# Projecting the first half of the queries before the second half is normalised, with the split of the weights shared by two engines

## The reference

```
x: (8, 128, 512)                      # 8 tiles of 128 tokens, 1024 tokens in all
xn = (x - mean(x)) / sqrt(var(x) + 1e-5)
q  = xn @ Wq                          # Wq: (512, 1024), so q: 1024 tokens x 1024
kv = context @ Wkv                    # Wkv: (512, 2048)
x  = x + softmax(clip(mask(q k^T / 8))) v @ Wo + bo
```

## Time and profile before

| what | value |
|---|---|
| runs | 3358.84, 3362.94, 3366.79 us (median 3362.94) |
| profiled execution | 3363.22 us, span 3361.2 us |
| PE, DVE, ACT, POOL busy | 93%, 74%, 51%, 52% of the span |
| mean granted clock of TensorE | 0.97 of full speed |

### The profile page before, as it was taken

One profiled execution on the slowest core, in us unless ns is written; L12 is line 12 of the kernel. 1 busy time (PEld: TensorE's weight loads), 2 busy tenths in 40 slices (PEclk: granted clock), 3 DMA queues, 4 the chain that ended last, 5 costly groups with the idle time before them and its releaser, 6 DMA issues. The chain is left out here.

```text
span 3361.2 us, 50813 instructions
## 1 busy us (share of the span) xinstructions
PE 3135.3 (93%) x18068; PEld 2664.4 (79%) x18068; DVE 2480.7 (74%) x3447; ACT 1728.2 (51%) x3283; POOL 1744.6 (52%) x1122
## 2 busy tenths in 40 slices
PE   5999999999999999999999996988989877899996
PEld 4788888888888888888888885867767655678996
DVE  4699999999999999999999996685675754523213
ACT  3466666666666666666666663253453426211000
POOL 4365665566556566566555664141441436346663
PEclk9999999999999999999999997989999889899998
DMA  5544444454454445444454444100000120123220
GB/s 195 157 119 111 117 116 113 117 129 98 120 123 121 114 105 127 109 123 115 102 129 117 113 101 116 57 28 28 1 16 1 58 62 1 63 70 125 83 88 32
DMA packets 216084, 312.41 MB, mean 93 GB/s; under 512 B 28704, under 2 KB 122016, under 8 KB 207648
## 3 DMA queue, kind: packets, MB, share of 16 engines
q1 hardware_dynamic: 213024, 300.74, 34.3%
q0 software_dynamic: 2816, 8.46, 0.7%
HBM read 151.75 MB, written 23.13 MB: 52 GB/s over the span
## 5 line engine op out<-in xcount | busy, mean ns | idle before, releaser
L480 POOL TENSOR_TENSOR es<-es,e 128x512 f32<-128x512 f32 x480 | 621.7, 1295 | 741.6 <-ACT e L556 741.6
L645 DVE TENSOR_TENSOR e_hl<-e,e_hl 128x512 fp32r<-128x512 f32 x512 | 679.7, 1327 | 0.3 <-ACT e L556 0.3
L489 POOL TENSOR_TENSOR c_lo<-raw,c_hi 128x512 fp32r<-128x512 f32 x248 | 427.0, 1722 | 0.0
L636 DVE TENSOR_SCALAR sc<-ps_s,top 128x512 f32<-128x512 f32 x512 | 384.6, 751 | 55.7 <-ACT e L556 1.4
L715 PEld LDWEIGHTS ps_s<-q_hl,k_hl 128*128 128x128 f32 x2048 | 308.6, 190 | 67.7 <-issue 28.5
L632 DVE TENSOR_TENSOR ps_s<-ps_s,right 128x512 f32<-128x512 f32 x512 | 353.4, 690 | 9.1 <-ACT right L565 7.8
L715 PE MATMUL ps_s<-q_hl,k_hl 128*128 128x256 f32 x2048 | 330.9, 284 | 15.4 <-DVE sc L636 15.4
L665 PE MATMUL ps_p<-c_hi,wa 128*128 128x512 f32 x1024 | 339.1, 392 | 4.5 <-PEq L115 4.5
L665 PE MATMUL ps_p<-wa,c_hi 128*128 128x512 f32 x1024 | 337.8, 391 | 0.0
L676 PE MATMUL ps_o<-e_hl,v_hl 128*128 128x256 f32 x2048 | 331.1, 284 | 3.3 <-DVE e_hl L645 3.3
L552 ACT ACTIVATE e_hl<-sc 128x512 fp32r<-128x512 f32 x512 | 324.7, 634 | 1.4 <-PE ps_o L676 1.0
(11 more groups left out here) (395 smaller groups left out, 7371.7 us busy)
## 6 DMA issues: line engine op xcount, KB each, us to landing
k_hl<-ot SPq DMA_DIRECT2D x1024, 128.0 KB, 2.8
raw<-in_ctx_t SPq DMA_DIRECT2D x64, 1024.0 KB, 6.4
raw<-in_L_ffn_W_experts SPq DMA_DIRECT2D x64, 256.0 KB, 2.9
q_hl<-q_hi_scratch SPq DMA_DIRECT2D x32, 256.0 KB, 5.5
q_hl<-q_lo_scratch SPq DMA_DIRECT2D x32, 256.0 KB, 6.3
raw<-in_L_xattn_Wkv SPq DMA_DIRECT2D x8, 512.0 KB, 4.9
q_hi_scratch<-qa_qh SPq DMA_DIRECT2D x16, 256.0 KB, 2.5
q_lo_scratch<-qa_ql SPq DMA_DIRECT2D x16, 256.0 KB, 3.4
```

Source lines behind the costliest of these rows:

```text
L480: g.tensor_tensor(ES[:, GL], ES[:, GL], e, ALU.add).then_inc(summed, 1)
L489: g.tensor_tensor(C_lo[:, n % 2, k, :], RAW[:, n % 2, k, :], C_hi[:, n % 2, k, :].bitcast(F32), ALU.subtract).then_inc(clo_done, 1)
L636: v.tensor_scalar(SC[:, s % 2].rearrange("p (j q) -> p j q", j=GRP), halves[:, :, 0, :], top[:, i * (M // P) + kt16:i * (M // P) + kt16 + ...
L645: v.tensor_tensor(E2[:, s % 2, :, 1, :], E[:, s % 2].rearrange("p (j q) -> p j q", j=GRP), E2[:, s % 2, :, 0, :].bitcast(F32), ALU.subtrac ...
```

## The change

In `stage_queries`:
- VectorE's program becomes: first half (`norms(0)`, `turned_lo(0)`), the low part of Wq piece 1 (which was GpSimd's), `norms(1)`, low parts of query groups 0 and 1, `turned_lo(1)`, groups 2 to 15.
- TensorE transposes tiles 0 to 3, computes groups 0 and 1, transposes tiles 4 to 7, and computes groups 2 to 15. `qa_pst` and `qa_psq` have four banks each.
- ScalarE puts its copies in a matching order, and the splits of pieces 4 to 7 stand after groups 3, 5, 8 and 10 (before: after 0, 2, 4 and 6).
- On SyncE's queue the loads of pieces 4 to 7 stand after the stores of groups 0, 2, 5 and 7 (before: 4 and 5 ahead of all stores, 6 after store 1, 7 after store 3).

In `rsqrt_cols`, for all stages: one instruction more ahead of the refinements, and three instead of four in each refinement, or two where y has a single column.

```
-    for n in range(3):
-        c.link(v.tensor_tensor(tmp, y, y, ALU.mult))
-        c.link(v.tensor_tensor(tmp, tmp, x, ALU.mult))
-        c.link(v.tensor_scalar(tmp, tmp, -0.5, 1.5, ALU.mult, ALU.add))
-        c.link(v.tensor_tensor(y, y, tmp, ALU.mult))
+    c.link(v.tensor_scalar(x, x, -0.5, None, ALU.mult))
+    for n in range(3):
+        if y.shape[-1] == 1:
+            c.link(v.scalar_tensor_tensor(out=tmp, in0=y, scalar=y, in1=x, op0=ALU.mult, op1=ALU.mult))
+        else:
+            c.link(v.tensor_tensor(tmp, y, y, ALU.mult))
+            c.link(v.tensor_tensor(tmp, tmp, x, ALU.mult))
+        c.link(v.scalar_tensor_tensor(out=y, in0=tmp, scalar=1.5, in1=y, op0=ALU.add, op1=ALU.mult))
...
+        QR, QB, HB = 3, 4, B // 2
...
+        SPLIT_LOADS = {0: 4, 2: 5, 5: 6, 7: 7}
+        SPLITS = {3: 4, 5: 5, 8: 6, 10: 7}
+        TURNS_AFTER = 1
...
             def load(n):
-                if n >= 2:
-                    sp.wait_ge(lo_split, n - 1)
+                if n == 3:
+                    sp.wait_ge(wq_lo_second, 1)
+                elif n >= 2:
+                    sp.wait_ge(lo_split, max(n - 2, 1))
...
-            for n in range(2, 6):
-                load(n)
-            store(0)
-            store(1)
-            load(6)
-            store(2)
-            store(3)
-            load(7)
-            for n in range(4, NQ):
+            load(2)
+            load(3)
+            for n in range(8):
+                store(n)
+                if n in SPLIT_LOADS:
+                    load(SPLIT_LOADS[n])
+            for n in range(8, NQ):
                 store(n)
...
         def _(g):
-            for n in range(NP):
+            for n in (0, *range(2, NP)):
...
+            norms(0)
+            turned_lo(0)
+            v.wait_ge(hi_split, 2)
+            for hi, lo, src in parts_of(1):
+                v.tensor_tensor(lo, src, hi.bitcast(F32), ALU.subtract).then_inc(wq_lo_second, 1)
+            norms(1)
             for n in range(NQ):
                 v.wait_ge(hi_done, n + 1)
...
+                if n == TURNS_AFTER:
+                    turned_lo(1)
...
             split(0)
+            turned_hi(0)
+            turned_hi(1)
             split(1)
-            for b in range(B):
-                turned_hi(b)
+            turned_hi(2)
+            turned_hi(3)
             split(2)
             split(3)
...
-                if n in (0, 2, 4, 6):
-                    split(4 + n // 2)
+                if n == TURNS_AFTER:
+                    for b in range(HB, B):
+                        turned_hi(b)
+                if n in SPLITS:
+                    split(SPLITS[n])
...
+            turn(0)
+            t_.wait_ge(lo_split, 1)
+            t_.wait_ge(wq_lo_second, 1)
             for n, (c, t) in enumerate(GROUPS):
-                if n >= 2:
-                    t_.wait_ge(lo_done, n - 1)
+                t_.wait_ge(xt_lo, (t + 1) * HB)
+                if n >= QB:
+                    t_.wait_ge(lo_done, n - QB + 1)
...
+                if n == TURNS_AFTER:
+                    turn(1)
```

More of the change, by code:

```diff
@@ L129, in stage_queries @@
         QL_ = sb("ql", [P, QR, 512], F32R)
[L130 to L131 removed]
+        ps_t = ctx.enter_context(nc.psum_tensor("qa_pst", [P, HB, 512], F32))
+        ps_q = ctx.enter_context(nc.psum_tensor("qa_psq", [P, QB, 512], F32))
         ident_in, raw_in, x_in = sem("ident_in"), [sem("raw_in0"), sem("raw_in1")], [sem(f"x_in{b}") for b in range(B)]
[L134 removed]
+        hi_split, lo_split, wq_lo_second = sem("hi_split"), sem("lo_split"), sem("wq_lo_second")
         vchain, normed, turned, xt_hi, xt_lo = sem("vchain"), sem("normed"), sem("turned"), sem("xt_hi_done"), sem("xt_lo_done")
@@ L208, in _, with norms @@
             c = Chain(v, vchain, 0, 0)
-            for hb in range(2):
-                bs = range(hb * HB, (hb + 1) * HB)
+            def norms(hb):
+                bs, s_ = range(hb * HB, (hb + 1) * HB), slice(hb * HB, (hb + 1) * HB)
                 for b in bs:
@@ L218, in _, with turned_lo @@
                     v.tensor_scalar(X[:, b], X[:, b], mom[:, b, 0:1], rs[:, 1, b:b + 1], ALU.subtract, ALU.mult).then_inc(normed, 1)
-                for b in bs:
+            def turned_lo(hb):
+                for b in range(hb * HB, (hb + 1) * HB):
                     v.wait_ge(xt_hi, b + 1)
                     t_ = slice(b * P, (b + 1) * P)
-                    v.tensor_tensor(XT_lo[:, :, t_], ps_t[:, b % 2].rearrange("p (k f) -> p k f", k=KC), XT_hi[:, :, t_].bitcast(F32),
+                    v.tensor_tensor(XT_lo[:, :, t_], ps_t[:, b % HB].rearrange("p (k f) -> p k f", k=KC), XT_hi[:, :, t_].bitcast(F32),
                                     ALU.subtract).then_inc(xt_lo, 1)
+            norms(0)
[4 more added lines that the diff above has]
+            norms(1)
             for n in range(NQ):
                 v.wait_ge(hi_done, n + 1)
-                v.tensor_tensor(QL_[:, n % QR, :], ps_q[:, n % 2, :], QH[:, n % QR, :].bitcast(F32), ALU.subtract).then_inc(lo_done, 1)
+                v.tensor_tensor(QL_[:, n % QR, :], ps_q[:, n % QB, :], QH[:, n % QR, :].bitcast(F32), ALU.subtract).then_inc(lo_done, 1)
+                if n == TURNS_AFTER:
+                    turned_lo(1)
         @block.scalar
@@ L237, in turned_hi @@
                 a.wait_ge(turned, b + 1)
-                a.copy(XT_hi[:, :, b * P:(b + 1) * P], ps_t[:, b % 2].rearrange("p (k f) -> p k f", k=KC)).then_inc(xt_hi, 1)
+                a.copy(XT_hi[:, :, b * P:(b + 1) * P], ps_t[:, b % HB].rearrange("p (k f) -> p k f", k=KC)).then_inc(xt_hi, 1)
             split(0)
+            turned_hi(0)
+            turned_hi(1)
             split(1)
-            for b in range(B):
-                turned_hi(b)
+            turned_hi(2)
+            turned_hi(3)
             split(2)
@@ L248, in _ @@
                     a.wait_ge(q_out[n % QR], 32 * (n // QR))
-                a.copy(QH[:, n % QR, :], ps_q[:, n % 2, :]).then_inc(hi_done, 1)
-                if n in (0, 2, 4, 6):
-                    split(4 + n // 2)
+                a.copy(QH[:, n % QR, :], ps_q[:, n % QB, :]).then_inc(hi_done, 1)
+                if n == TURNS_AFTER:
[3 more added lines that the diff above has]
+                    split(SPLITS[n])
         @block.tensor
@@ L255, in _, with turn @@
             t_.wait_ge(ident_in, 16)
[L256 to L264, removed]
+            def turn(hb):
+                for b in range(hb * HB, (hb + 1) * HB):
+                    t_.wait_ge(normed, b + 1)
+                    if b >= HB:
+                        t_.wait_ge(xt_lo, b - HB + 1)
+                    for k in range(KC):
+                        mm = t_.transpose(ps_t[:, b % HB, k * P:(k + 1) * P], X[:, b, k * P:(k + 1) * P], I[:])
+                    mm.then_inc(turned, 1)
+            turn(0)
+            t_.wait_ge(lo_split, 1)
+            t_.wait_ge(wq_lo_second, 1)
             for n, (c, t) in enumerate(GROUPS):
-                if n >= 2:
-                    t_.wait_ge(lo_done, n - 1)
+                t_.wait_ge(xt_lo, (t + 1) * HB)
+                if n >= QB:
+                    t_.wait_ge(lo_done, n - QB + 1)
                 m = 0
@@ L270, in _ @@
                     for w, x_ in ((WQ_lo, XT_hi), (WQ_hi, XT_lo), (WQ_hi, XT_hi)):
-                        mm = t_.matmul(ps_q[:, n % 2, :], w[:, k, c * P:(c + 1) * P], x_[:, k, t * 512:(t + 1) * 512],
+                        mm = t_.matmul(ps_q[:, n % QB, :], w[:, k, c * P:(c + 1) * P], x_[:, k, t * 512:(t + 1) * 512],
                                        start=m == 0, stop=m == 3 * KC - 1)
```

3 lines of the change are left out of this document (removed).

## The result

The change took 3338.28 us (median of 4 runs, 3334.97 to 3341.87) against 3362.81 us of the kernel before (4 runs, 3358.84 to 3366.79): a ratio of 0.9928, interval 0.9914 to 0.9943, so 24.5 us (19 to 29) faster. The prediction had 3345.3 and a range of 3339 to 3354, so the measured time lies 0.7 us outside it. The profiled execution took 3334.97 us, its span is 3333.0 us, 28.2 less than before's. The next stage's first matmul stands at 83.19 instead of 98.40: 15.2 us come from the first stage, where 14.7 were forecast. The other 13.0 us lie behind it, where step 5 had 3.2.

What follows compares the result with a forecast made beforehand. TensorE, busy 93% of the span, was taken as the bound, so gains come only where it stands still. 14.7 us (first stage) plus 3.2 (rsqrt_cols elsewhere) made 17.9: 3363.2 - 17.9 = 3345.3 us, range 3339 to 3354.

Steps and rivals of the forecast that it cites:

- step 5: Shorter rsqrt_cols in later stages: ten wide calls at 0.2 us, two narrow at 0.6; 3.2 us saved, bounds 0 and 5.8.
- Step 1: First stage, first half: without GpSimd's second subtraction VectorE goes on; tile 3 normalised at about 17.1, low part ends 19.75.
- Step 2: First stage: Wq piece 1's low part on VectorE takes 2.3 us; group 0 starts at 22.1, 17.2 us earlier.
- Step 3: First stage, second half: GpSimd's subtractions lock VectorE's normalising chain, costing 6.2 us; TensorE waits from 30.2 to 35.6.
- Step 4: First stage, groups 2 to 15: four banks keep stalls to 1.0 us; body ends at 79.2, 14.7 us saved.
- The lock bit: Rival, first stage's second half: the lock bites less, 3 to 5 us more gained, 3340 to 3342; 17%.
- the later loads: Rival, groups 2 to 15: later loads or stores hold ScalarE, 4 to 9 us lost, 3349 to 3354; 19%.
- the body did not stretch: Rival, first stage: head shortened but body stretches by as much; within 6.7 us of before; 6%.
- the clock rival: First stage: clock stays at 1.2 GHz after TensorE's pause; all 14 groups cost 34 us, net slower (3379); 4%.

Runs made afterwards that it cites:

- e6: The change with the low part of Wq piece 1 back on GpSimd, order of halves, banks and queues kept; 3333.2 us (0.9915).
- e4: The change with GpSimd taking piece 2 only when all 8 tiles are normalised; 3332.3 us (0.9914).
- e5: The change with two PSUM banks instead of four for the query groups (QB = 2); 3341.6 us (0.9949).
- e7: The kernel before with the new rsqrt_cols in every stage but the first; 3351.0 us, gain 8 us (4 to 12).
- e12: The kernel before with the new rsqrt_cols in all later stages but stage_attend; 3350.4 us, gain 6 us (3 to 9).
- e2: The kernel before with the new rsqrt_cols alone, in all stages; 3352.7 us (0.9973).
- e9: e4 with GpSimd's first subtraction (Wq piece 0) also waiting, until the first half is normalised; 3325.1 us (0.9902).
- e15: e9 run again, unchanged; 3329.0 us (0.9907).

## Why the prediction was right where it was, and wrong in the size

*Step 1, first half.* Right: the normalising ended at 16.9 (forecast 17.1), the low parts at 19.4 (19.75).

*Step 2, piece 1 on VectorE.* The cost was right (2.28 us, forecast 2.3), group 0 at 21.74 (22.1). The gain came, 17.6 us for the 17.2 forecast, but not by the move: e6 starts group 0 at 21.31 without it. Step 1 wanted GpSimd's second subtraction gone so that VectorE could go on; in e6 it ran, and VectorE's low parts began at 16.81 all the same, as in the change (16.85).

*Step 3, the lock on the second half.* Right in size, partly wrong in kind. The pause was 5.93 us and ended at 36.13 (forecast 5.4 us, ending at 35.6). e4, without it, is 8.7 us faster in the stage, where the step had 5.4: there TensorE also transposes at full pace, 1.9 instead of 3.7 us, and the matmuls behind them run at full pace (0.23 us apart from the second on). Wrong was which instructions are held. The step took all four with one tensor input as free, from a row of a single column. With four columns they are not: L220 took 1.21 and L77 2.32 us beside GpSimd. The chain was held four times, not three. It cost little, since what counts is when GpSimd's last subtraction ends: 34.1 (forecast 33.6). The Trainium skill, page "SBUF — State Buffer", section "Who interferes with whom", says that tensor_scalar too can enter a mode that takes the port pair shared with GpSimd; these two rows agree with it, and the 0.15 of the single column would fit its not being entered there; no row names the mode.

*Step 4, groups 2 to 15.* Right: the last group's matmul at 78.3 (body end 78.7, forecast 79.2), no stall of TensorE where 1.0 was allowed. The reason given, the four banks, was too strong as far as e5's profile goes: ScalarE waited 2.1, 0.4 and 1.6 us for the pieces in the change, and with two banks TensorE stalled for 1.3 us.

*Step 5, `rsqrt_cols` elsewhere.* This is the step that failed: 3.2 us, where the rows give 5.6. It is a term that was mis-sized. The new form, `scalar_tensor_tensor`, was costed by a row of 0.227 us. In the change it takes 0.16 us where its scalar is a constant; only the other kind, whose scalar is a column of memory, takes 0.22:

```profile
2073.41 0.16 DVE L86 SCALAR_TENSOR_TENSOR t_col<-t_col 128x1 f32<-128x1 f32 x1
2073.61 0.22 DVE L82 SCALAR_TENSOR_TENSOR t_col<-t_col 128x1 f32<-128x1 f32 x1
```

A wide call therefore loses two instructions of 0.20 each, 0.4 us and not 0.2. A one-column refinement takes 0.45 us (two in 0.90, from 2073.16 to 2074.06) instead of 0.77 (two in 1.54): 0.8 a call with the instruction more ahead of it, and not 0.6. The wait in `stage_front` shows just that, 3.9 us for two calls and now 2.3. So 10 x 0.4 + 2 x 0.8 = 5.6 us, close to the step's upper bound of 5.8, and the measured idle time says 5.8. Choosing the row by its operation's name, when the one in the earlier trace rows has another kind of scalar, cost 2.4 us of the forecast.

That the totals agree so well is in part luck. Stage by stage, from the first matmul of one to that of the next, TensorE's idle time (mean of the four profiles without the new code there less that of the nine with it) fell by 0.8 us in `stage_dense`, as worked out (2 x 0.4), by 0.9 in `stage_front` (1.6) and 0.9 in `stage_project` (1.6), by nothing in `stage_attend` (0.4) and by 0.2 in `stage_cross` (no call), but by 3.0 in `stage_ffn_attend` (1.2). There a wait that the step did not list, for ScalarE, is shorter; before, then the change:

```profile
PE g_ps L1743 <- ACT g_s L1600: 5.9, 1, 5.9
```

```profile
PE g_ps L1769 <- ACT g_s L1626: 4.3, 1, 4.3
```

It is 5.9 or 6.0 us in all six profiles with the old code in that stage, and 4.4 or less in all eleven with the new. What shortens it by 1.6 us no run here shows.

*The sum.* The forecast is 7.0 us above the measured median: 2.4 to 2.6 from step 5, 0.5 from the first stage (15.2 for 14.7), 0.4 because the sum started from the profiled 3363.2 and not from the median, and 3.5 for which the sum has no term. Step 5 at its right size would have made it 3342.9, inside the range; the 3.5 us took it below 3339. The 21.0 us that the first stage and step 5 account for lie inside the measured interval of 19 to 29. The sum put the clock behind the first stage at nothing, and TensorE's busy time there scatters by 6 us for one kernel; the profiled pair had 5.9 us of it. Whether the change also runs a little longer at full clock is open: the means of the profiles say up to 4.8 us, most of it due to which executions were profiled, and the intervals of the parts (e7, e12) ask for none.

*The rivals.* The lock bit as forecast; the later loads held ScalarE for 4.1 us in three waits and TensorE for none, where the rival had 4 to 9 lost; the body did not stretch. After the pause of 5.93 us TensorE was at half pace for the transposes, and so were the first four matmuls behind them (0.57 to 0.42 apart); all 168 of the 14 groups took 39.2 us, 0.233 each against 0.227 at full pace, so the clock rival did not come true.

## What to carry to other kernels

When two engines lock each other out for a whole instruction, a chain of tiny dependent instructions is the worst thing to put beside long ones: each 0.16 us link can cost 2.3. Holding the long instructions back with a wait until the chain is done costs nothing if their results have slack: here two such waits gave 7 to 9 us, and moving work between the two engines gave nothing. Before crediting a moved piece of work, check that what waited for it was not waiting for something else anyway. And when a profile pair differs over a long stretch, split the stretch into TensorE's idle and busy time: in these 17 profiles the idle time went with the code, and the busy time of the same matmuls with the clock, which scatters.

## What the runs showed of the hardware beyond that

- A one-input instruction on 128x4 elements is held by GpSimd's subtraction (1.21 and 2.32 us), one on 128x1 is not (0.15).
- How far ahead VectorE starts matters: 1.66 us ahead of GpSimd's first subtraction four normalising instructions took 1.92 us (e2), 1.38 us or less ahead at least 6.1 (e6: 6.18).
- `scalar_tensor_tensor` on a few columns takes 0.16 us with a constant and 0.22 us with a column as its scalar.
- One unchanged kernel (e9, e15) needed 3077.5 and 3071.6 us of TensorE's busy time for the same matmuls, with 176.7 and 160.7 us of low clock.
